# First pair of a four-block transformer kernel: sums of the ternary weights' magnitudes, ternary chunks and weight splits at other jobs

## What is computed

```python
x = x + _L0_xattn_ref(_layernorm(x), ctx, mask, mask, Wq, bq, Wk, bk, Wv, bv)   # 16 heads
x = x + _L0_ffn_ref(_layernorm(x), weight1, weight2, weight3)    # silu(a) * b, 1408 wide
x = x + _L1_xattn_ref(_layernorm(x), mask, ctx, ctx, wq, wk, wv, wo)   # one head, keys: context and x
x = x + _L1_ffn_ref(_layernorm(x), w1, w2, w3)                   # ternary weights, sigmoid(x1) * x2
return x

def _quantize(w):                       # of _L1_ffn_ref, for each of its three weights
    gamma = jnp.mean(jnp.abs(w))
    return jnp.clip(jnp.round(w / (gamma + 1e-8)), -1.0, 1.0)
```

## Time and profile before

| | us |
|---|---|
| median of 3 runs | 1415.34 |
| lowest and highest run | 1415.29, 1416.7 |
| the profiled execution | 1413.76 |
| its span, first to last instruction | 1411.9 |
| PE busy | 1300.1 (92%) |
| DVE busy | 1002.1 (71%) |
| ACT busy | 648.3 (46%) |
| POOL busy | 298.7 (21%) |

### The profile page before, as it was taken

One profiled execution on the slowest core, in us unless ns is written; L12 is line 12 of the kernel. 1 busy time (PEld: TensorE's weight loads), 2 busy tenths in 40 slices (PEclk: granted clock), 3 DMA queues, 4 the chain that ended last, 5 costly groups with the idle time before them and its releaser, 6 DMA issues.

```text
span 1411.9 us, 23348 instructions
## 1 busy us (share of the span) xinstructions
PE 1300.1 (92%) x9142; PEld 755.2 (53%) x9142; DVE 1002.1 (71%) x1523; ACT 648.3 (46%) x941; POOL 298.7 (21%) x473
## 2 busy tenths in 40 slices
PE   5798979999999899978999999999999999999998
PEld 2343413232232223226676667777767877777776
DVE  8989889889888888874858846635466444675353
ACT  5675648888887888862632111231111311112210
POOL 1008446456466465200000000000000000000000
PEclk9999989999999999989999999999999999999999
DMA  6300223343343332236533101100010000100000
GB/s 195 120 19 16 87 66 98 108 115 99 110 122 113 108 102 95 61 133 215 175 118 124 62 31 61 31 1 1 31 62 16 16 1 31 61 1 31 1 1 31
DMA packets 78038, 101.23 MB, mean 72 GB/s; under 512 B 14679, under 2 KB 51647, under 8 KB 77927
## 3 DMA queue, kind: packets, MB, share of 16 engines
q1 hardware_dynamic: 75879, 99.43, 22.5%
q0 software_dynamic: 2048, 0.27, 0.1%
HBM read 78.07 MB, written 21.34 MB: 70 GB/s over the span
## 4 chain that ended last, share of the span: by engine, by line
PE 40%; DVE 9%; DMA 2%; ACT 1%; issue 1%; POOL 1%; POOLq 0%; DVEq 0%; ACTq 0%; SPq 0%
PE double L1823 13%; PE double L1837 11%; PE double L1849 5%; PE double L1902 3%; PE double L1870 3%; PE double L1859 3%; PE double L1889 1%; DVE stats L2010 1%; PE double L1807 1%; DVE f1w L2115 1%; DVE hid L2057 1%; DMA x_early<-scr_x 1%; DVE gate L2055 1%; DMA out_x<-x_early 1%; DVE x_early L2026 1%
## 5 line engine op out<-in xcount | busy, mean ns | idle before, releaser
L1049 ACT ACTIVATE prob<-level,head_scale 128x512 f32<-128x512 f32 x512 | 318.1, 681 | 73.4 <-PE level L947 71.7
L1411 DVE TENSOR_REDUCE nmx<-level 128x2 f32<-128x1024 f32 x256 | 306.8, 1220 | 46.9 <-PE level L937 46.4
L1935 ACT ACTIVATE th<-double 128x512 f32<-128x512 f32 x96 | 53.9, 561 | 386.4 <-PE double L1823 213.4
L947 PE MATMUL level<-stacks 59*128 59x512 f16 x512 | 174.2, 390 | 10.3 <-ACT prob L1049 10.2
L1996 POOL TENSOR_TENSOR rstd<-meanvar,halfpow 128x2 f32<-128x2 f32 x22 | 15.2, 689 | 691.0 <-DVE meanvar L2016 691.0
L374 PE MATMUL level<-prob,x_parts 128*128 128x512 bf16 x540 | 125.9, 389 | 35.9 <-ACT prob L326 16.2
L1823 PE MATMUL double<-x_parts,f0w 128*128 128x256 f16 x1408 | 157.1, 275 | 1.7 <-PEq L522 1.6
L937 PE MATMUL level<-stacks 57*128 57x512 f16 x512 | 151.3, 389 | 6.1 <-DVE nmx L1411 6.0
L1823 PE MATMUL double<-x_parts,f1w 128*128 128x256 f16 x1408 | 155.2, 273 | 0.3 <-DVE hid L2057 0.3
L1823 PEld LDWEIGHTS double<-x_parts,f0w 128*128 128x128 bf16 x1408 | 138.6, 99 | 20.9 <-issue 2.5
L1823 PEld LDWEIGHTS double<-x_parts,f1w 128*128 128x128 bf16 x1408 | 137.6, 98 | 18.4 <-DVE hid L2057 0.6
(11 more groups left out here) (257 smaller groups left out, 1858.1 us busy)
## 6 DMA issues: line engine op xcount, KB each, us to landing
stacks<-scr_q SPq DMA_DIRECT2D x64, 96.0 KB
stacks<-scr_k SPq DMA_DIRECT2D x64, 96.0 KB
hid<-in_f1w1t SPq DMA_DIRECT2D x8, 704.0 KB, 6.8
hid<-in_f1w2t SPq DMA_DIRECT2D x8, 704.0 KB, 4.3
inputs<-in_x SPq DMA_DIRECT2D x8, 512.0 KB, 7.7
inputs<-in_ctx SPq DMA_DIRECT2D x8, 512.0 KB, 7.2
scr_q<-splits SPq DMA_DIRECT2D x16, 256.0 KB, 2.4
scr_k<-splits SPq DMA_DIRECT2D x16, 256.0 KB, 2.3
```

The costliest lines, as they stand in the source:

```text
L947: nc.tensor.matmul(pB[n % 2], Ks[rows, g, j // 2, P * c:P * (c + 1)], Qs[rows, g, j // 2, :], start=True, stop=True).then_inc(s["b_pe"], 1)
L1049: nc.scalar.activation(prob[:, c, j, :], pB[(64 * b + 16 * g + 4 * c + j) % 2], ACT.Exp, scale=hscale[:, 10:11]).then_inc(s["exp_done"], 1)
L1411: nc.vector.tensor_reduce(nmx[:, g % 2, :, half, tt], pA[(32 * b + 8 * g + u // 2) % 2], AX.X, ALU.max, negate=True).then_inc(s["max_done" ...
L1935: y = nc.scalar.activation(th[:, 0:m, :], src[:, 0:m, 0:S], ACT.Tanh, scale=0.5 / XS)
```

## The change

Three lists of the first pair are set anew, and the place of one reduce.

```diff
-        SUM_AFTER = [3, 4, 5, 6, 8, 9, 10, 11, 12, 13, 14, 16]
-        MAKE_BEFORE = [("s", 1, 0, 0), ("k", 1, 1, 0), ("q", 1, 1, 0), ("v", 1, 1, 0), ("s", 1, 1, 0), ("av", 1, 0, 0),
-                       ("wo", 1, 0, 0), ("wo", 1, 1, 0), ("up", 2, 0, 0), ("up", 2, 0, 1), ("up", 2, 0, 2), ("up", 2, 0, 3)]
-
-        SPLIT_AFTER = {8: "k", 9: "q", 10: "v", 11: "o"}
+        SUM_AFTER = list(range(3, 15))
+        MAKE_BEFORE = [("q", 1, 0, 0), ("v", 1, 0, 0), ("turn", 1, 1, 0), ("s", 1, 0, 0), ("k", 1, 1, 0), ("q", 1, 1, 0),
+                       ("v", 1, 1, 0), ("s", 1, 1, 0), ("av", 1, 0, 0), ("wo", 1, 0, 0), ("wo", 1, 1, 0), ("up", 2, 0, 0)]
+
+        SPLIT_AFTER = {8: "k", 9: "q", 11: "v", 14: "o"}
...
-                    if isinstance(it, int) and it == 0 and job == ("v", 1, 0, 0):
+                    if isinstance(it, int) and it == 0 and job == ("down", 0, 1, 0):
                         magnitude_sums()
```

## The result

| | before | changed |
|---|---|---|
| median of the runs, us | 1416.7 (5 runs) | 1424.92 (5 runs) |
| lowest and highest | 1415.29, 1418.67 | 1420.75, 1429.42 |
| profiled execution, its span | 1413.76, 1411.9 | 1420.75, 1418.9 |
| dense block, from its first product to the end of the span | 766.7 | 771.4 |

The ratio is 1.0054, 95% interval 1.0036 to 1.0072: the changed kernel is slower by 5.1 to 10.2 us. The forecast of 1421.1 with a range to 1425.0 holds the median, close to its upper end. The profiled executions differ by 7.0 us, and 2.25 of these lie ahead of the dense block, where nothing was changed: its first product starts at 645.21 before and at 647.46 after.

What follows compares the result with a forecast made beforehand. PE bounds the kernel, except for three first-pair gaps ended by late DVE results. Job 26 10.7 us late less 4.9 back at job 39 gives +5.8: 1419.6 us for the profiled execution, median 1421.1, range 1417.0 to 1425.0.

Steps and rivals of the forecast that it cites:

- part 1: Jobs 8 to 15: gap before job 15 falls to 0.9 us, no clock dip, job 15 ends 3.0 us earlier.
- T: Point when SP may ask for the sums, after DVE's second context split: 719.8, row sums 0.4 us later at 720.2.
- Part 3, the round trip: Row sums at 720.2, broadcast at 723.0, chunk 0 8.7 us later; PE stands 11.2 us before job 20.
- The second gap: Wait before job 21 for the low half of job 19: +3.9 us, scores perhaps 1.7 us slower hiding in it.
- Job 26: Starts at 766.3 against 755.62, 10.7 us late, after the waits before jobs 20 and 21.
- job 25's gap: The PE gap of 1.20 us before the scores of sequence 1 goes: -1.2 us.
- Part 4: Jobs 32 to 39: one chunk left of four, job 39 starts right behind job 38, 4.9 us back.
- The short round trip: Rival: chunk 0 lands 4.0 us after issue instead of 8.7 behind the broadcast; sum +1.2, 1416.5 us; chance 0.09.
- The covered wait: Rival: sum and chunk 0 are there when DVE has done k's low half; -4.7, 1410.6 us; chance 0.06.
- my heavier form: Rival: transfers delay the first split and the clock falls again behind the second gap; +8.6, 1423.9 us; chance 0.20.

Runs made afterwards that it cites:

- the splits alone: The kernel before with only the splits of v and o moved (jobs 11 and 14), sums and chunks at old places: median 1414.8 us, ratio 0.9987.
- the kernel with the chunks back: The changed kernel with the ternary chunks back at their old jobs, the rest as changed: median 1416.28 us against 1416.79 before, ratio 0.9998.
- the kernel with the row sums alone in the queue: Against the changed kernel: chunks at other places, two reloads before the row sums are reduced, both context loads behind the broadcast; 1409.81 us, ratio 0.9954 to before.
- the second of the two stores: The changed kernel with the row sums stored twice, the second store waiting for the first: dense block 774.5 us, only execution 1422.36 us.
- the kernel with the row sums first: The changed kernel with row sums, broadcast and reloads of chunks 0 and 1 sent before the last context load: median 1415.13 us, ratio 1.0002 to before.

## Why the prediction was right, and where it was off

- **What bounds it, part 1.** Right. Gap 1.15 us (0.98 in the trace that has all 44 records) for 0.9, no fall of the clock, and the product of job 15 ends 3.5 us sooner than before, counted from the start of the block, for 3.0. As said, this alone bought nothing, since PE then waits for q.
- **Part 2, T.** Right. The second context split began 72.5 us into the dense block, it ended at 73.8, and the row sums' store came at 74.2; the working has them at 74.6 (719.8 - 645.2) and 75.0 (720.2 - 645.2). The wait for the high half of o delayed DVE's part of job 15 as described, with 2.02 us of idling.
- **Part 3, the round trip.** The mechanism held, and so nearly did its total, but two terms in it were off against each other. Row sums to broadcast took 3.70 us, above the 2.8 taken and above the upper end of 3.3: the store came out as slow as the whole context load in front of it. Broadcast to chunk 0 took 7.35 us, less than the 8.66 of the first trace of before, from which the 8.7 was taken. The other traces of before show 7.42 and 9.05, the splits alone 7.09, the four traces of the changed kernel 7.14 to 7.35. So this step isn't a fixed 8.7: here it was 1.3 us shorter, and why it is long in two traces of before is open. Together the two steps took 11.05 us for 11.5 (10.7 to 10.9 in the other three traces). The gap before job 20 was 10.47 us for 11.2. The store's 3.70 lies outside the range that I gave this term (2.2 to 3.3), and the forecast held because the two misses nearly cancelled, which is luck and not skill.
- **The second gap.** 1.77 us where the sum has 3.9 less up to 1.7 for slow scores. The scores were slow by 1.5, the case that the working leaves at "perhaps". From job 20 to job 21 PE took 8.69 us for the 8.8 forecast, since DVE's work between the two low halves sets it.
- **Job 26** started 9.3 us late for 10.7: job 15 ended 3.45 us sooner, the wait before job 20 adds 10.47, the stretch from there to job 21 takes 3.45 more than before, and the 1.20 of job 25 goes. The working has 3.0, 11.2, 3.9 and 1.2 for them; its 0.2 of rounding is the end of job 15, put at 707.7 in part 1 and at 707.9 in part 3. The term for job 25's gap was shaky too: of three traces of before, two show it (1.20, 1.25) and one doesn't.
- **Part 4.** Right. All four traces of the changed kernel start job 39 without a gap, all three of before have 3.2 to 3.6 us and the low clock there. That the fall of the clock comes with it can't be counted on: the second trace of the kernel with the chunks back has the gap and not the fall. The first trace alone gives +4.2 us at job 40 for the +5.8 forecast, and the four against three +5.1 for the whole block.
- **The rivals.** The short round trip did not happen. The trace shows 11.05 us from row sums to chunk, not the 6.1 us that the fit of the Trainium skill ("DMA: Bandwidth & Descriptors", "Anatomy of one DMA") would give (an estimate). The page gives its fit for transfers that GpSimd issues, and these are SP's. The broadcast alone took 4.5 to 5.8 us from issue to landing in every trace. The covered wait did not happen either, but the kernel with the row sums alone in the queue shows how it can be had: it took a request that doesn't stand behind the second context split, as the rival said, and no chunk ahead of q's low half.
- **The size.** The forecast of +5.8 agrees with the traces' +5.1. The timed +8.2 is near my heavier form (+8.6), but its mechanism, a later first split and a second fall of the clock, is in none of the four traces to more than 0.9 us. So the median fell into the range, 0.1 us from its end, for a reason that I can't show in full, and that is luck in part.

## What to carry to other kernels

Before work is moved earlier, follow its inputs to the queue that brings them: here twelve chunks were moved three to six jobs ahead, while the store and the broadcast that they need stood behind a load that waits for a later point of another engine. A small transfer that a whole engine waits for belongs ahead of the large ones, and requests whose data nobody hurries for belong behind it. A gain ahead of a wait that is set elsewhere only makes the wait longer, so look for the last arrival first. And before a few us are put down to an edit, compare several traces: here the same kernel's executions differed by up to 7 us ahead of the code that was changed.

## What the runs showed of the hardware

- A store of 1.5 KB took 1.8 to 2.2 us from its issue to the broadcast's when nothing large was in front of it (the second of the two stores, also with nothing large in front, took 2.99), 3.5 to 4.0 behind one context load of 512 KB, and 6.59 behind a context load and two chunks. By the Trainium skill ("DMA: Bandwidth & Descriptors", "Queues, rings and completion order") each DMA engine consumes its ring in order; these times agree with that.
- The broadcast of 1.5 KB to 128 partitions took 4.55 us (725.59 to 730.14) with a context load and no reload behind it, 4.5 likewise in the kernel with the row sums alone in the queue, and 5.2 to 5.8 with two reloads behind it.
- In the gap of 10.47 us the granted clock fell to 0.50, the level of 1.2 GHz, while PE did nothing, and was back about 3 us after it had begun to work; the scores took 6.9 us. Behind the gap of 4.23 us in the kernel with the row sums first it stayed low for 5.5 us of work, and the scores took 8.1 us instead of 5.4. Gaps of 2.57 and 3.17 us brought a fall in one trace and none in another of the same kernel. What a gap costs in clock isn't fixed by its length.
- Identical code ahead of the dense block took between 645 and 652 us, and in the seven traces of the two kernels the later starts go with more time at the lower clock (about 50 us at 645.2, 66 at 652.2); in the other kernels' traces they do so less closely.
